# Second attention layer of a four-layer kernel: transfers split by head, the xT copy moved to VectorE, constant rows written by DMA, and the first maxima of a batch four slots later

## The reference, cut to what matters

```
H = 16; Dh = C // H                                  # 16 channels a head
Q, K, V = proj(Wq), proj(Wk), proj(Wv)
att = einsum('bhqd,bhkd->bhqk', Q, K) / sqrt(Dh) + b[0]
att = att * m + (1 - m) * NEG_INF                    # m: the key mask of the batch
y = einsum('bhqk,bhkd->bhqd', softmax(att), V)
out = x + y                                          # heads side by side in the 256 channels
```

## Time and profile before

| | |
|---|---|
| median of three runs | 3043.02 us |
| the profiled execution | 3042.79 us, span 3041.0 us |
| busy over the span | TensorE matmul 2689.0 us (88%), VectorE 1971.6 (65%), ScalarE 1245.7 (41%), POOL 635.5 (21%) |
| mean granted TensorE clock | 0.959 |
| start of `l3_part` | about 1981.8 us into the span, so it takes some 1059 us |
| DMA issues within it | all on the SP queue |

### The profile page before, as it was taken

How to read it: one execution, slowest core, us unless ns; L and a number is a source line. 1 busy time by engine, 2 the same in 40 slices (tenths; PEclk the granted TensorE clock), 3 DMA queues, 4 the chain that set the end, 5 groups by cost and what they waited for, 6 DMA issues and landing times. The chain is left out here.

```text
span 3041.0 us, 116061 instructions
## 1 busy us (share of the span) xinstructions
PE 2689.0 (88%) x48668; PEld 1509.0 (50%) x48668; DVE 1971.6 (65%) x3754; ACT 1245.7 (41%) x1939; POOL 635.5 (21%) x736
## 2 busy tenths in 40 slices
PE   6999999999599999999999999938888888888882
PEld 2333333333288888888888888812222222222220
DVE  4555555555677777777777775458766667666660
ACT  1454454444211111111111111105777767777774
POOL 0000000000011222122222221143334343433432
PEclk8999999999799999999999999969999999999997
DMA  1310110110100000000000000023434443444432
GB/s 49 99 51 25 49 48 26 49 46 19 37 5 0 0 1 0 1 0 0 0 1 0 1 0 0 1 62 79 109 103 120 115 110 108 119 110 109 120 82 69
DMA packets 120464, 146.38 MB, mean 48 GB/s; under 512 B 23758, under 2 KB 76912, under 8 KB 120348
## 3 DMA queue, kind: packets, MB, share of 16 engines
q1 hardware_dynamic: 116892, 138.77, 16.5%
q10 hardware_dynamic: 3456, 6.29, 0.7%
HBM read 100.60 MB, written 44.40 MB: 48 GB/s over the span
## 5 line engine op out<-in xcount | busy, mean ns | idle before, releaser
L1357 DVE TENSOR_REDUCE x<-exp_ps 128x2 f32<-128x1024 f32 x352 | 427.1, 1222 | 200.6 <-PE exp_ps L1460 200.6
L839 PE MATMUL exp_ps<-region,gru_hT 128*16 128x128 f32 x16384 | 498.4, 274 | 55.1 <-DVE gru_hT L922 44.8
L839 PEld LDWEIGHTS exp_ps<-region,gru_hT 128*16 128x16 f32 x16384 | 428.3, 103 | 122.7 <-DVE gru_hT L922 122.7
L1303 ACT ACTIVATE region<-exp_ps,x 128x1024 f32<-128x1024 f32 x336 | 370.3, 1109 | 89.5 <-PE exp_ps L1435 89.5
L539 DVE TENSOR_REDUCE l_maxes<-exp_ps 128x2 f32<-128x1024 f32 x176 | 215.3, 1224 | 223.4 <-PE exp_ps L605 221.0
L864 ACT ACTIVATE gru_r<-exp_ps 128x128 f32<-128x128 f32 x256 | 71.2, 278 | 623.2 <-PE exp_ps L839 623.2
L770 POOL TENSOR_TENSOR xT<-xT,gru_hT 128x64 f32 (+1 forms) x256 | 133.6, 522 | 912.1 <-DVE gru_hT L922 896.0
L891 DVE SCALAR_TENSOR_TENSOR xT<-x,condT,xT (+1 forms) x420 | 318.4, 801 | 0.0
L1448 PE MATMUL bank<-region,x 128*17 128x512 f32 x2048 | 282.0, 624 | 8.7 <-ACT region L1303 5.3
L824 PE MATMUL exp_ps<-region,gru_x_st 128*32 128x128 f32 x8192 | 285.8, 273 | 0.0
L839 PE MATMUL bank<-region,gru_hT 128*16 128x128 f32 (+1 forms) x8192 | 270.5, 273 | 0.0
(11 more groups left out here) (166 smaller groups left out, 3886.7 us busy)
## 6 DMA issues: line engine op xcount, KB each, us to landing
region<-key_query_scratch SPq DMA_DIRECT2D x128, 192.0 KB
l_rden<-rden_scratch SPq DMA_DIRECT2D x64, 256.0 KB
key_query_scratch<-x SPq DMA_DIRECT2D x48, 256.0 KB, 2.9
key_query_scratch<-region SPq DMA_DIRECT2D x48, 256.0 KB, 2.5
l_out<-x_scratch SPq DMA_DIRECT2D x64, 192.0 KB
l_xin<-in_x SPq DMA_DIRECT2D x16, 512.0 KB, 4.2
l_rden<-rden_scratch SPq DMA_DIRECT2D x128, 64.0 KB, 2.0
l_xres<-in_x SPq DMA_DIRECT2D x16, 512.0 KB, 3.7
```

Source lines behind the costliest of these rows:

```text
L839: last = pe.matmul(out[QW * j:QW * j + rows, cols], hT[:, p, k, state], group_of(wh[:, k, gate, :], j), start=False, stop=True, skip_group ...
L1303: act.activation(probs[:, 2 * (seg % 2) + hp, :, :], pairs[ring.place[2 * slot]][:, :, :], ACT.Exp, scale=factors[:, 2:3])\
L1357: dve.tensor_reduce(maxes[:, half, qt, head % HH:head % HH + 2], pairs[ring.place[2 * slot + 1]][:, :, :], AX_X, ALU.max).then_inc(taken[" ...
```

## The change

It does seven things in `l3_part`, and one in `setup_part`:

- `load_rden` and `load_x3` issue one DMA for each head of a group (four each) of 16 partitions, instead of one DMA of 4 x 32 rows and two of 96 and 16. The partitions between the heads are no longer loaded; POOL sets them once at the start (`out_sb` whole to 0, `rden_bc` whole to 1).
- The copy of xT into `xs` goes from POOL to VectorE, ahead of its slot 0.
- The rows of `UNIT` come from a DRAM tensor `g.unit`, which `setup_part` writes, by four DMAs at the start (`load_units`); the two POOL memsets are gone. TensorE waits for them before its first step.
- `FIRST = 4`: the maxima tiles of a batch run from slot 4 to slot 3 of the next step (`tile_at`), instead of slot 0 to 31.
- `AT` is written anew: each of the sixteen task parts has one even slot of its own. mtb moves from slot 1 to 4, mta from 17 to 20, `xn` to 2 and 6, q to 8 to 14, k to 16, 18, 22, 24, v to 26, 28, 30 and slot 0 of the next step; the ScalarE parts of q and k move from slots 13 and 21 to 15 and 25.
- On POOL the finish of group 2 goes ahead of the mta split.
- On SP `load_x3` of groups 2 and 3 goes from behind `load_stack` half 0 to right behind `load_rden` of group 3, and `store_out` of group 2 from behind the denominators of group 2 to ahead of the max rows of half 0. `store_max_rows` is cut in two functions that are called one after the other.

```
-    AT = {("mtb", 0): 1, ("xn", 0): 2, ("xn", 1): 4, ("q", 0): 6, ("q", 1): 10, ("k", 0): 14, ("mta", 0): 17, ("k", 1): 18,
-          ("v", 0): 22, ("v", 1): 26}
+    AT = {("xn", 0): ((2, 2),), ("mtb", 0): ((4, 0),), ("xn", 1): ((6, 2),), ("q", 0): ((8, 2), (10, 2)), ("q", 1): ((12, 2), (14, 2)),
+          ("k", 0): ((16, 2), (18, 2)), ("mta", 0): ((20, 1),), ("k", 1): ((22, 2), (24, 2)), ("v", 0): ((26, 1), (28, 1)),
+          ("v", 1): ((30, 1), (0, 0))}
+    Q_PART1, K_PART1, RECIPROCAL = 15, 25, 8
+    FIRST = 4
...
+        def tile_at(slot):
+            return (slot - FIRST) % SLOTS, 0 if slot < FIRST else 1
...
             def load_rden(grp, count):
                 wait(sp, scaled, count)
-                sp.dma_start(rden_bc[:, grp % 2, :], g.rden_dram[GH * grp:GH * grp + GH, :]
-                             .rearrange("j (o n) -> j o n", o=1).broadcast_to([GH, QW, T])).then_inc(rden_loaded[grp % 2], 16)
+                for j in range(GH):
+                    h = GH * grp + j
+                    sp.dma_start(rden_bc[QW * j:QW * j + D3, grp % 2, :], g.rden_dram[h:h + 1, :].broadcast_to([D3, T]))\
+                      .then_inc(rden_loaded[grp % 2], 16)
...
-                windows = bass.AP(tensor=rows.tensor, offset=rows.offset, ap=[[D3 * T, GH - 1], [T, QW], [1, T]])
-                sp.dma_start(out_sb[0:QW * (GH - 1), grp % 2, :], windows).then_inc(x3_loaded[grp % 2], 16)
-                sp.dma_start(out_sb[QW * (GH - 1):QW * (GH - 1) + D3, grp % 2, :], rows[D3 * (GH - 1):D3 * GH, :])\
-                  .then_inc(x3_loaded[grp % 2], 16)
+                for j in range(GH):
+                    h = GH * grp + j
+                    sp.dma_start(out_sb[QW * j:QW * j + D3, grp % 2, :],
+                                 g.x3_dram[bass.ds(s, 1), h * D3:h * D3 + D3, :].rearrange("o r n -> (o r) n"))\
+                      .then_inc(x3_loaded[grp % 2], 16)
...
                     store_out(s - 1, 1, n(4, -2))
                     load_rden(3, n(4, -2))
+                    load_x3(s - 1, 2, n(16, 0), n(128, -64))
+                    load_x3(s - 1, 3, n(16, 0), n(128, -64))
...
                 if active(s, 0):
                     store_den(par, 1, n(4, 2))
+                if active(s, -1):
+                    store_out(s - 1, 2, n(4, -1))
                 if active(s, 1):
-                    store_max_rows(1 - par, 0, n(2, 3), n(32, 32), n(32, 48))
+                    store_max_rows(0, n(2, 3), n(32, 32))
+                    load_max_rows(1 - par, 0, n(32, 48))
...
+            def load_units(rows, w):
+                n = rows.stop - rows.start
+                for hf in range(2):
+                    units = bass.AP(tensor=g.unit.tensor, offset=g.unit.offset, ap=[[0, n], [0, 2], [T, HH], [1, T]])
+                    sp.dma_start(stack[HALF * hf + rows.start:HALF * hf + rows.stop, :, w, :, :], units).then_inc(units_loaded, 16)
...
         def _(pool):
-            for hf in range(2):
-                pool.memset(stack[HALF * hf + QW:HALF * hf + HALF, :, :, :, :], UNIT).then_inc(const_ready, 1)
-                pool.wait_ge(const_ready, hf + 1)
...
-                    pool.tensor_copy(xs[:, :, :], g.xT[:, :, bass.ds(b, 1), :].rearrange("p k o t -> p k (o t)")).then_inc(xs_in, 1)
...
                 if active(s, 2):
                     split(1, 2 * (s + 2))
+                if active(s, -1):
+                    finish(s - 1, 1 - par, 2)
                 if active(s, 1):
                     split_max(2 * (s + 1), "mta", s + 2)
                 if active(s, 2):
                     split(0, 2 * (s + 2) + 1)
                 if active(s, -1):
-                    finish(s - 1, 1 - par, 2)
                     finish(s - 1, 1 - par, 3)
...
         @block.vector
                 for slot in range(SLOTS):
+                    if slot == 0 and active(s, 2):
+                        wait(dve, ready["xn"], 2 * (s + 2))
+                        dve.tensor_copy(xs[:, :, :], g.xT[:, :, bass.ds(s + 2, 1), :].rearrange("p k o t -> p k (o t)")).then_inc(xs_in, 1)
```

More of the change, by code:

```diff
@@ L43 @@
 CHUNKS = C // CW
+UNIT = 2.0 ** 11
 def wait(eng, sem, value):
@@ L1058, in load_stack, with store_max_rows @@
                                  g.rows3[0:4, bass.ds(s, 1), :].broadcast_to([4, HH // 2, T])).then_inc(stack_loaded[half], 16)
-            def store_max_rows(par, half, made, read, stored):
+            def store_max_rows(half, made, read):
                 wait(sp, mp_done, made)
@@ L1308, in step @@
                         evac_sums(s, par, (slot - 9) // 8)
-                    for kind, idx in AT:
-                        if AT[kind, idx] + 2 * (PARTS.get(kind, 1) - 1) == slot and active(s, OFF[kind]):
+                    for kind, idx, part, last, off in parts_at(slot):
+                        if last and active(s, off):
                             evac(s, par, kind, idx)
@@ L1348, in step @@
                         dve.reciprocal(den_c[:, :], den_c[:, :]).then_inc(recip_done, 1)
-                    if active(s, 1):
-                        head, qt = 2 * (slot // TC), slot % TC
+                    tile, off = tile_at(slot)
+                    if active(s, off):
+                        head, qt = 2 * (tile // TC), tile % TC
                         half = head // HH
-                        if slot % 16 == 0:
-                            wait(dve, ready["mta" if half == 0 else "mtb"], s + 1)
-                        wait(dve, ready["max"], SLOTS * (s + 1) + slot + 1)
+                        if tile % 16 == 0:
+                            wait(dve, ready["mta" if half == 0 else "mtb"], s + off)
+                        wait(dve, ready["max"], SLOTS * (s + off) + tile + 1)
                         dve.tensor_reduce(maxes[:, half, qt, head % HH:head % HH + 2], pairs[ring.place[2 * slot + 1]][:, :, :],
@@ L1459, in maxima, with task @@
                     rows = slice(HALF * hf, HALF * hf + KMAX)
-                    last = pe.matmul(pairs[ring.place[2 * slot + 1]][:, hf, :], stack[rows, 1 - par, 1, h, qt * P:qt * P + P],
-                                     stack[rows, 1 - par, 0, h, :], start=True, stop=True)
+                    last = pe.matmul(pairs[ring.place[2 * slot + 1]][:, hf, :], stack[rows, of, 1, h, qt * P:qt * P + P],
+                                     stack[rows, of, 0, h, :], start=True, stop=True)
                 last.then_inc(ready["max"], 1)
-            def task(s, par, kind, idx, part):
+            def task(s, par, kind, idx, part, done, off):
                 n = next(n for n, t in enumerate(one.tasks) if t[1:3] == (kind, idx))
-                out, parts = task_ps, PARTS.get(kind, 1)
+                out = task_ps
                 if part == 0:
@@ L1481, in task @@
                     kt = 2 * idx + part
+                    of = par if off == 0 else 1 - par
                     for c in range(CC):
[L1483 removed]
+                        last = pe.matmul(out[:, part * C:part * C + C], xn[:, of, c, kt * P:kt * P + P], w_sb[:, 2, c, :],
                                          start=(c == 0), stop=(c == CC - 1))
@@ L1497, in step @@
                         scores(s, par, slot)
-                    if active(s, 1):
+                    if active(s, tile_at(slot)[1]):
                         maxima(s, par, slot)
-                    for kind, idx in AT:
-                        for part in range(PARTS.get(kind, 1)):
-                            if AT[kind, idx] + 2 * part == slot and active(s, OFF[kind]):
-                                task(s, par, kind, idx, part)
+                    for kind, idx, part, last, off in parts_at(slot):
+                        if active(s, off):
+                            task(s, par, kind, idx, part, last, off)
                     if slot % 2:
```

77 lines of the change are left out of this document (43 added, 34 removed).

## The result

The changed kernel takes 2927.14 us (median of 4 runs, 2926.38 to 2927.91), the kernel before 3044.63 beside it: a ratio of 0.9616 (0.9601 to 0.9631). The profiled execution took 2927.91 us, with a span of 2926.1 and a mean granted TensorE clock of 0.976 (before 3041.0 and 0.959). Between the two profiled executions the gain is 114.9 us, where the forecast had 113.

A forecast was written before the change was run, and what follows sets the result against it. It took one circle of SP's loads and stores, POOL's finishes and the stack load as the bound. Gains of 19 + 6 + 1 + 77 + 10 - 0.3 = 113 us off 3042.8 gave 2930 us, range 2905 to 2972.

The forecast's parts named there:

- the circle: Steps 1 to 13: chain from mtb over SP's loads, POOL's finishes, max rows, keys and stack to next maxima; 52.9 us a step.
- TensorE's own pace: Steps 1 to 13: the other limit, step 0's 52.6 us less 1.2 for mtb and mta, 51.4 us a step.
- The start: Start of the part: without POOL's memsets first transposes at about 1994 instead of 2013, gain 19 us (15 to 20).
- Step -1 and step 0: First steps: fewer VectorE reductions and no stack wait, 6 us (0 to 8); mtb and mta off full slots, 1 us.
- Denominators' wait: Sign to look for: VectorE's wait in slot 8 for denominators read back, under 1 us.
- Residual loads at more than 0.5 of the DMA engines: Sign to look for: residual loads by head keep over 0.5 of the DMA engines busy, landing in 2 us.
- The end: Slot 0 of step 14 to the end: 126.4 us instead of 136.4, gain 10 us.
- A: Rival: TensorE is the bound, small landings overlap better, 21 us more gained, 2909 us; chance 0.22.
- B: Rival: the circle is longer, 0.5 us on each of six landings, steps 56.0 us, 2969 us; chance 0.18.
- C: Rival: VectorE's copy meets POOL's lock and waits for one finish, +1.2 us a step, 2945 us; chance 0.07.
- D: Rival: the copy's wait moves elsewhere whole, steps stay at 58.95 us, only the ends gain, 3007 us; chance 0.10.
- E: Rival: slower, each load by head costs SP 0.75 us to issue instead of 0.43, steps 63 us, 3059 us; chance 0.05.

The follow-up runs named there:

- the best kernel: The changed kernel with the f16 part of q in slot 18 (was 15), of k in 26 (25), denominators' reciprocal in 10 (8): 2916.93 us.

## Why the prediction was right, point by point

The forecast was 2930, the measurement 2927.14, and no stage is off by more than 4 us. Inside the steps, where most of the gain lies, one term and the choice of the limit were wrong: the circle was put 0.6 to 1.0 us too long and TensorE's own pace 1.0 too short. That the steps came out within 0.1 us is luck in part.

**What bounded the kernel before: right.** The circle over residual loads, finishes, max rows, keys and stack was the bound: step by step before, 50.55 from mtb to stack, 7.75 to the first maxima and 1.13 to the next mtb are the 59.4 us of that step. Loads by head alone gave 84.8 us and the group loads put back in cost 102 (3029.0 - 2927.1). That the copy stands "at its end" was right as well, and the price of it as a wait of TensorE was nothing: moved alone it gave 0.0, moved back it cost nothing. Two readings were loose. The clock of 0.68 is that of the microsecond from 2373; where the sum matmuls of 1.84 us run, from 2375 to 2376, it is 0.50. And the 16.01 us at the finish of group 2 are more than half a matter of SP's order, as shown above.

**The start: 19 predicted.** Six small row operations "at 0.6 us each" take 0.41 to 0.68, the copy 0.67 for 0.6, and the transposes came at 1993.89 for 1994. The first of these rows is the very operation that took 13.94 us before, the second the copy (timeline of VectorE, changed kernel):

```profile
1990.28 0.53 DVE L1432 TENSOR_SCALAR x<-x 16x512 f32<-16x512 f32 x1
...
1993.07 0.67 DVE L1371 COPY x<-xT 128x1024 f32<-128x1024 f32 x1
```

With POOL's memsets gone, so is the hold on VectorE. That this hold was POOL's work on the same port, as the Trainium skill has it in "SBUF — State Buffer", "Who interferes with whom", fits, but no run separates it from other causes. It was no hold on all of VectorE: beside the same memset its reductions of 128 x 512 at the start of the part took 1.27 us for two, as in the changed kernel.

**Step -1 and step 0: 6 + 1 predicted, 4.1 measured** (23.3 less the 19.2 of the start). From the first transposes to slot 0 of step 0 it is 65.0 us for 70.1, so step -1 gave 5.1 of its 6. Step 0, slot 0 to slot 0, takes 56.0 for 55.0 and lost 1 where it should have gained 1. At the last maxima of step -1 and in slot 0 of step 0 TensorE waits for VectorE (1.94 and 1.11 us, at 2058.67 and 2060.39), and the granted clock from 2060 to 2070 is 0.51. I had counted the tasks saved and not what TensorE does with the first slots of scores, exponentials and maxima together.

**Steps: 53.0 predicted, 52.96 measured, by the wrong one of the two limits.** The circle was forecast at 52.9 as 51.7 to the first stack DMA, 7.75 to usable, less 6.5. It is 44.66 from mtb to stack (forecast 51.7 - 6.8 = 44.9), 6.9 to 7.3 to usable and 0.3 to the mtb: 51.9 to 52.3. "TensorE's own, 51.4" was the mis-sized term: it took step 0 of the kernel before (52.6), less two tasks' savings. Step 0 is shorter than a steady step at this pace: with loads by head alone it is 52.8, the steady ones 53.9. In the changed kernel ScalarE's pieces on one spot (a pair of 4.12 us) and VectorE ahead of mta (3.82) are part of the difference. Undisturbed steps of the changed kernel take 52.4 to 52.5. So both limits lie within some 0.6 us of each other, TensorE's the longer one, where the forecast had the circle longer by 1.5, and the stack shows as a wait of TensorE only twice (0.39 and 1.10 us, in steps 2 and 4). The best kernel takes 51.8 by spreading those pieces and meets the circle; with slot 3 or slot 0 the circle sets the step.

**Denominators' wait "under 1 us": too low.** It is 0.40 to 2.12, and once 3.12 (timeline of VectorE, then what TensorE makes of it):

```profile
2182.98 0.55 DVE L1382 RECIPROCAL x<-x 128x64 f32<-128x64 f32 x1 [3.12 <-DMA x<-den_scratch]
```

```profile
2184.67 0.39 PE L1471 MATMUL bank<-region 55*128 55x512 f16 x2 [1.97 <-DVE x L1392]
...
2187.49 1.91 PE L1484 MATMUL bank<-region,x 128*17 128x512 f32 x8
```

The sum matmuls behind it take 1.91 us and not 1.05, and that step takes 55.49. The prediction's second turn of the circle gave 52.0 for a step of 52.9, a margin of 0.9 us; with steps of 52.4 and a queue that varies by a microsecond, that is none.

**"Residual loads at more than 0.5 of the DMA engines": wrong** (0.20 to 0.23). I took it that a load by head can use all 16 engines and forgot my own price of its issue: 32.8 KB each 0.45 to 0.49 us is 67 to 73 GB/s. The chain counted the issues, so the sum was right while the sign to look for was not. The rule of the Trainium skill, "DMA: Bandwidth & Descriptors", "Why a DMA increments its semaphore by 16 and not by 1", with which the trace of before agrees (0.19 x 16 = 3.0), fits the result as well: cut so that each DMA has 16 or 32 rows, the loads land in 1.7 to 2.0 us, whether they have 32 or 64 KB. That three engines carried the windows is not shown by itself: the share is a mean over all sixteen, and it reads nearly the same under the loads by head.

**The end: 10 predicted, 13.8 measured.** From the last store of denominators (2895.06) to the end it is 31.0 us, forecast 31.3, before 37.4. Of the other 7.4 step 14, slot 0 to slot 0, gives 6.1 (49.4 for 55.5; forecast 50.5), where VectorE waits 0.40 us for the denominators and not 4.73, and step 15 up to its last denominators gives 1.3 (42.2 for 43.6; forecast 44.6).

**The rivals.** A (2909) did not come, though the best kernel gets near its step (51.8 for 51.4) by another way. B did not come, C neither (the copy takes 0.68 us in slot 0), D is what the copy alone does, and E's issue of 0.75 us did not occur: 0.45 to 0.49.

It stays open how far the circle could be shortened further: a second queue beside SP's, or the finishes on another engine, were not tried.

## What to carry to other kernels

In a pipeline that closes on itself, the wait that the profile shows longest is only the place where the circle's length comes out: removed alone it comes back elsewhere, at the same step. Write the circle down term by term, shorten the term that has no reason for its length (here a group's residuals, 9.1 us in windows and 3.3 by head), and then look at how near the engines' own pace is, since here the two limits take over from each other within some half a microsecond. A first use of a loaded buffer should stand as far behind the start of its chain as the order of work allows: one slot earlier cost 36 us on the best kernel, four slots earlier 118 on the changed one, while with the start of the chain (mtb) in slot 1 a first use in slot 0 cost nothing.

## What the runs showed of the hardware

- A load of 32 KB costs SP 0.45 to 0.49 us in a loop of eight and lands in 1.7 to 1.8 us; one of 64 KB lands in 1.9 to 2.0. Under eight loads of 32 KB the profile shows 66 GB/s, about what their issue alone allows (67 to 73); with 64 KB each the same number of issues carries twice the bytes, and the kernel takes the same time.
- A wait of TensorE costs more than its length, here about a third more. With the first maxima in slot 0, the wait of 6.45 us is followed by 5 us at a granted clock of 0.50, scores of 0.61 us for 0.39 and sum matmuls of 1.91 for 1.05. I had priced such waits at their length alone and was 37 us short over the kernel; 14 steps of 2.3 us are 32 of these.
- Two operations of VectorE on 16 x 512 f32 take 0.41 and 0.53 us with POOL idle, and took 6.20 and 13.94 beside POOL's memset; its two reductions of 128 x 512 took 1.27 us either way.
